# A graph layer in one kernel: node rows loaded a second time with features on partitions, their scale from a norm on TensorE, keys of block 0 and stores of counts placed earlier

## The chip, the core and the metric

One core of one Trainium2 chip. The metric is the device time of the kernel in microseconds (us), median of three runs.

## The reference, cut to what matters

6250 nodes with 128 features each, 200000 edges sorted by destination, float32. Two message layers with a residual and a normalisation each:

```python
edge_index = jnp.stack([src, dst])
h = x @ W + b_W;  xi, xj = jnp.split(h, 2, axis=-1)
xji = (xj[senders] + edge_features @ W_e + b_We) / (in_degree[receivers][..., None] + 1e-06)
x = _layernorm(x + xi + segment_sum(xji, receivers))          # layer 0
out = segment_sum(h1[src] * norm[:, None], dst) + b           # layer 1, h1 = x @ W1, self loops added
x = _layernorm(x + leaky_relu(batch_norm(out)))
```

## The kernel before

Nodes are cut into 25 blocks of 256 (`NB`), a block into 16 slots of 16 destination nodes (`SL`; the last block has 7). The gather of neighbours is a matrix product. For each slot VectorE writes one-hot tiles from the edge keys (`one_hots`, lines 616 and 619, one call for two slots, in a ring of six slots), TensorE multiplies them into counts of edges by source and destination (`count`, line 858), and ScalarE copies the counts from PSUM to SBUF (`pair_out`, line 1065, two PSUM buffers). One block later TensorE multiplies x by the counts of the whole block (`product`, line 876); one more block later come the messages, the normalisation and the second layer's first part. Edge features are summed by `edges` (line 895). Behind the 25 blocks a second sweep reads the stored counts back (`gather_z`).

x is used as two float16 halves (`xsplit`, made by `split_high` on ScalarE, line 1130, and `split_low` on VectorE, line 681). Their scale is a power of two that is read off the largest magnitude of x: `largest` (line 646, three pieces of x), `scales`, `spread_scales`. Ahead of that, x times its own weights, the own part, is made in 13 groups of up to four 128x128 tiles: `turn_x` transposes a group on TensorE (line 972), ScalarE copies it out (line 1137), `own_product` multiplies (line 981, one PSUM buffer), ScalarE copies the result into `zown` (line 1142). Groups 0 to 3 come before block 0, the others one a slot in block 0.

Work is ordered by hand. The loop `for b in range(NB + 2)` over blocks, with `for s in range(SL)` over slots inside, is written once for each engine, and each engine runs its own instructions strictly in that order, with semaphores between them. SyncE (SP) issues nearly all transfers in one queue: for a block the destination rows of block b+4 (`load_rows`), eight start values read into registers, eight small loads of edge destinations, a store of the degrees' inverse, the store of the counts of block b-1 (`keep_counts`, line 349), then the edge features in two groups (`load_edges`, line 342). Group 1 of block 0 goes into the memory where x lies, so it waits until x is split. Counts have two buffers: slot 0 of block b waits until the counts of block b-2 are stored (`counts_kept`, line 1061).

The start of a block among the sorted edges is found from destination rows: `float_rows` on ScalarE, `find_below` and `pick_rows` on VectorE, `find_rows` on TensorE, `count_row` and `start_of` on VectorE. GpSimd then gathers the block's keys (`windows`), VectorE decodes them (`make_keys`), TensorE turns them (`turn_keys`, line 921), ScalarE copies them (`tables`, line 1089).

## Time and profile before

| | |
|---|---|
| median of 3 runs | 938.35 us (937.87 to 938.45) |
| profiled execution | 936.68 us, of which the span is 934.6 us |
| TensorE busy | 883.9 us, 95% |
| VectorE busy | 676.6 us, 72% |
| ScalarE busy | 450.3 us, 48% |

The 2.1 us between the time and the span lie around the first and last recorded instruction. Shares of the whole span hide stages: the first two blocks take until about 82 us, the 25 blocks until about 715 us, and VectorE has nearly all its work in them.

### The profile page before, as it was taken

How to read it: one execution, taken by the hardware profiler on the slowest of the kernel's cores; microseconds unless marked ns; L12 is line 12 of the kernel's file. 1: busy time of each engine (PE TensorE's matmuls, PEld its weight loads, DVE VectorE, ACT ScalarE, POOL GpSimd, SP SyncE). 2: the span in 40 equal slices, each digit the busy share in tenths (PEclk: the TensorE clock that was granted, in tenths of full speed). 3: DMA queues.
4: the chain of work that ended last, by engine and by line, in shares of the span. 5: the costliest groups of instructions: out<-in, count | busy, mean ns of one | idle time of the engine just before them, and what ended most of it. 6: DMA issues, size and time to landing. Idle time of an engine off the chain costs nothing.

```text
span 934.6 us, 30500 instructions
## 1 busy us (share of the span) xinstructions
PE 883.9 (95%) x12210; PEld 791.2 (85%) x12210; DVE 676.6 (72%) x1249; ACT 450.3 (48%) x983; POOL 349.4 (37%) x401
## 2 busy tenths in 40 slices
PE   4867999999999999999999999999999999999995
PEld 4756888888988898989899999999988888888874
DVE  6999899999999998899888899888842111112255
ACT  3764666656666665556565556565542000000026
POOL 2236444455554444455334455434332011112200
PEclk8988999999999999999999999999999999999998
DMA  6428999998879788777878758678667897779654
GB/s 180 110 83 296 361 345 320 317 342 290 313 247 319 284 311 283 229 229 241 253 264 277 223 185 301 214 274 282 209 216 299 343 358 279 272 260 326 249 155 136
DMA packets 96762, 244.77 MB, mean 262 GB/s; under 512 B 39560, under 2 KB 64838, under 8 KB 90726
## 3 DMA queue, kind: packets, MB, share of 16 engines
q1 hardware_dynamic: 95014, 239.46, 73.7%
q0 software_dynamic: 1600, 3.28, 1.4%
q8 instruction: 100, 1.64, 0.8%
q14 instruction: 48, 0.39, 0.2%
HBM read 183.85 MB, written 58.85 MB: 260 GB/s over the span
## 4 chain that ended last, share of the span: by engine, by line
PE 85%; DVE 5%; issue 3%; ACT 3%; DMA 1%; SPq 1%; ACTq 0%; DVEq 0%
PE x_ps L876 26%; PE pair_ps L951 19%; PE pair_ps L858 13%; PE e_ps L895 10%; PE x_ps L884 9%; PE j_ps L933 2%; PE j_ps L981 2%; DVE lo_oh L616 1%; DVE key_oh L619 1%; PE pair_ps L960 1%; PE j_ps L934 1%; ACT counts L1065 1%; PE u_vps L1409 1%; DMA counts_kept<-counts 1%; DMA streams<-in_x 1%
## 5 line engine op out<-in xcount | busy, mean ns | idle before, releaser
L1065 ACT CAST counts<-pair_ps 128x784 bf16<-128x784 f32 x391 | 315.3, 817 | 251.5 <-PE pair_ps L858 244.1
L876 PE MATMUL x_ps<-counts,xsplit 128*128 128x256 bf16 (+1 forms) x2450 | 307.5, 271 | 0.0
L616 DVE TENSOR_TENSOR lo_oh<-counter,lo_t 128x2048 bf16<-128x2048 bf16 x196 | 252.3, 1287 | 53.9 <-PE pair_ps L858 52.5
L876 PEld LDWEIGHTS x_ps<-counts,xsplit 128*128 128x128 f16 x2450 | 222.1, 98 | 29.3 <-issue 7.1
L858 PE MATMUL pair_ps<-key_oh,lo_oh 128*128 128x100 bf16 x3128 | 207.8, 209 | 22.5 <-ACT counts L1065 15.4
L858 PEld LDWEIGHTS pair_ps<-key_oh,lo_oh 128*128 128x128 bf16 x3128 | 182.8, 98 | 36.9 <-issue 15.0
L619 DVE TENSOR_TENSOR key_oh<-counter,key_t 128x1600 bf16<-128x1600 bf16 x196 | 196.4, 1002 | 0.0
L895 PE MATMUL e_ps<-streams 128*32 128x128 f32 x3528 | 106.9, 274 | 0.1
L884 PE MATMUL x_ps<-counts,zown 128*128 128x256 bf16 (+1 forms) x840 | 105.9, 269 | 0.1
L951 PE MATMUL pair_ps<-streams,zown 128*128 128x256 bf16 x878 | 99.0, 273 | 0.0
L895 PEld LDWEIGHTS e_ps<-streams 128*32 128x32 f32 x3528 | 93.3, 110 | 4.8 <-issue 1.0
L476 POOL TENSOR_SCALAR quot<-deg 128x2 f32<-128x2 f32 x25 | 5.7, 226 | 243.2 <-DVE junk L595 231.5
L951 PEld LDWEIGHTS pair_ps<-streams,zown 128*128 128x128 f16 x878 | 85.8, 98 | 11.4 <-issue 0.2
L884 PEld LDWEIGHTS x_ps<-counts,zown 128*128 128x128 f16 x840 | 76.1, 97 | 10.3 <-issue 2.9
L492 POOL TENSOR_SCALAR bias<-linear,share 128x128 f32<-128x128 f32 x50 | 76.0, 1532 | 14.7 <-DVE vo L705 13.7
L951 PE MATMUL pair_ps<-counts,zown 128*128 128x256 bf16 (+1 forms) x732 | 79.9, 268 | 0.0
L951 PEld LDWEIGHTS pair_ps<-counts,zown 128*128 128x128 f16 x732 | 69.3, 98 | 9.2
L1313 ACT ACTIVATE u_co<-u_co 128x1 f32<-128x1 f32 x1 | 0.2, 203 | 156.0 <-DVEq L1351 156.0
L825 DVE TENSOR_TENSOR s_mem<-pair_ps,key_oh 128x256 f32<-128x256 f32 (+1 forms) x23 | 9.6, 418 | 83.8 <-PE pair_ps L951 81.3
L639 DVE TENSOR_TENSOR streams<-iota,ekeys 128x1152 f32<-128x1152 f32 x49 | 67.5, 1377 | 2.7 <-PE e_ps L895 0.3
L833 DVE TENSOR_TENSOR xsplit<-pair_ps,key_oh 128x256 f32<-128x256 f32 (+1 forms) x25 | 10.5, 419 | 58.7 <-PE pair_ps L960 57.0
L507 POOL TENSOR_TENSOR streams<-streams,key_oh 128x512 bf16<-128x512 bf16 x13 | 15.0, 1151 | 84.9 <-DMA streams<-counts_kept 84.9
(181 smaller groups left out, 890.6 us busy)
## 6 DMA issues: line engine op xcount, KB each, us to landing
streams<-in_edge_attr SPq DMA_DIRECT2D x196, 576.0 KB, 9.1
counts_kept<-counts SPq DMA_DIRECT2D x10, 1600.0 KB, 9.1
streams<-counts_kept SPq DMA_DIRECT2D x6, 1600.0 KB, 6.5
counts<-counts_kept SPq DMA_DIRECT2D x4, 1600.0 KB, 7.1
counts_kept<-counts SPq DMA_DIRECT2D x2, 3136.0 KB, 12.7
streams<-counts_kept SPq DMA_DIRECT2D x2, 3136.0 KB, 14.8
edst<-in_dst SPq DMA_DIRECT2D x196, 4.5 KB
streams<-in_x SPq DMA_DIRECT2D x3, 1024.0 KB, 5.7
```

Source lines behind the costliest of these rows:

```text
L492: last = g.tensor_scalar(bias[:, t, :], bje, share[:, 2 * b + t:2 * b + t + 1], None, ALU.mult)
L616: dv.tensor_tensor(lo_oh[:, ring, :, :, :].rearrange("p r w k t -> p (r w) k t"), counter[:, :, :].unsqueeze(1).to_broadcast([P, g, P, 2]) ...
L619: dv.tensor_tensor(key_oh[:, ring, :, :, :].rearrange("p r w k t -> p (r w) k t"), counter[:, 0:KW, :].unsqueeze(1).to_broadcast([P, g, KW ...
L639: dv.tensor_tensor(e_oh[g][:, :, :], iota[:, 0:EC].unsqueeze(1).to_broadcast([P, EG * EJ, EC]), ekeys[:, k].unsqueeze(2).to_broadcast([P, ...
L858: last = nc.tensor.matmul(pair_ps[at % 2][:, half_of, col:col + KW], lo_oh[:, at % RING, w // 2, :, w % 2], key_oh[:, at % RING, w // 2, : ...
L876: last = nc.tensor.matmul(x_ps[:, 0, 0:n], xsplit[:, q // 2, q % 2, :], by_hi[:, q // 2, :], start=(q == 0), stop=(q == 2 * HS - 1))
L884: last = nc.tensor.matmul(x_ps[:, 1, 0:n], zsplit[:, z // 2, z % 2, :], by_hi[:, z // 2, :], start=(z == 0), stop=(z == early(k) - 1))
L895: last = nc.tensor.matmul(e_ps[EC * c:EC * (c + 1), g, :], e_oh[g][:, c * EJ + j, :], ebuf[g][:, c, j, :], start=(j == 0), stop=(j == EJ - 1))
L933: nc.tensor.matmul(out, sx[:, t:m:2], wj, start=True, stop=False)
L951: last = nc.tensor.matmul(z_ps[i % 2][:, 0:n], zsplit[:, q // 2, q % 2, :], by_hi[:, q // 2, :], start=(q == early(b)), stop=(q == 2 * HS ...
L981: last = nc.tensor.matmul(j_ps[:, k, :], xT[m % 2][:, k, :], wi, start=True, stop=True)
L1065: a.copy(out.rearrange("p h (g n) -> p h g n", g=2), pair_ps[at % 2][:, :, 0:4 * KW].rearrange("p g (n h) -> p h g n", h=HI)[:, 0:HS]).the ...
```

## The change

The host lays x out twice, without arithmetic: `x_rows` as before, nodes on partitions, and `x_columns`, features on partitions, both contiguous for each partition. `x_columns` is loaded into `zown`. `own_product` takes its tiles from there, with two PSUM buffers, and its result is copied over them; `turn_x` and `x_turned` are gone, and two groups instead of four come before block 0. The scale comes from the sum of squares of x instead of its largest magnitude: `sum_squares` multiplies the upper 16 bits of each tile by themselves on TensorE (49 products into one PSUM tile), `add_squares` takes the diagonal, one product with ones adds it up and spreads it. `largest` and `spread_scales` are gone; a check over rows (`row_largest`) moves to blocks 16, 18 and 20. The rows of blocks 2 and 3 are searched before the own weights are made ready, and `turn_keys(0)` no longer has four groups of x ahead of it. `keep_counts(b - 1)` is SP's first instruction of a block instead of standing behind the loads of starts and destinations. `count_row` and `start_of` stand two slots later.

```diff
-LARGEST_AT = (None, 2, 4)
-TOP_AT, SCALES_AT, SPREAD_AT = 5, 8, 12
-HIGH_AT, LOW_AT = (11, 13, 15), (16, 18, 20)
+NORM_AT, TOTAL_AT, SCALES_AT = 9, 9, 12
+HIGH_AT, LOW_AT = (11, 13, 15), (16, 18, 21)
+ROWS_CHECKED_AT = (16, 18, 20)
 OWN = [(h, min(4, HS - h)) for h in range(0, HS, 4)]
-OWN_FIRST = 4
+SQUARED_FIRST, OWN_FIRST = 4, 2
+SQUARED_IN = {2: (4, 5, 6, 7), 6: (8, 9, 10, 11, 12)}
...
+X_TOP = 15
+ROW_LEAST = 1.0
...
+def load_pieces(sp, out, table, loaded, pieces):
     for k in pieces:
...
+        at = piece_tiles(k)
+        sp.dma_start(out[:, at.start * F:at.stop * F], table[:, at.start * F:at.stop * F]).then_inc(loaded[k], 16)
...
-        few_ps = keys_ps[:, 2:4, :]
...
-        turn_ps = [x_ps[:, :, :].rearrange("p a (b n) -> p (a b) n", n=P), e_ps]
+        own_ps = [j_ps, e_ps]
+        squares_ps, norm_ps = x_ps[:, 0, 0:P], x_ps[:, 1, 0:1]
+        upper_halves = zown[:, :].bitcast(BF16).rearrange("p (h n q) -> p h n q", n=P, q=2)[:, :, :, 1]
...
-            sp.dma_start(wi, W0[:, 0:F]).then_inc(S["wi_in"], 16)
-            load_inputs(sp, {"x": xf}, x, S, range(1))
+            load_pieces(sp, columns, x_columns, S["columns_in"], range(1))
             for b in range(2, ROW_RING):
                 load_rows(sp, b)
+            sp.dma_start(wi, W0[:, 0:F]).then_inc(S["wi_in"], 16)
             load_weights(sp, {"wj": wj, "we": we, "bi": bi, "bj": bje, "be": be_t[:, :]}, W0, b0, We, be, S)
             sp.wait_ge(win_in[0], 32)
-            load_inputs(sp, {"x": xf}, x, S, range(1, len(X_PIECES)))
+            load_pieces(sp, columns, x_columns, S["columns_in"], range(1, len(X_PIECES)))
+            load_pieces(sp, xf, x_rows, S["x_in"], range(len(X_PIECES)))
...
-                    sp.wait_ge(S["x_turned"], len(OWN))
...
+                if 1 <= b <= NB - 2:
+                    keep_counts(b - 1)
                 if b + ROW_RING < LATE:
                     load_rows(sp, b + ROW_RING)
                 if b + ROW_RING == LATE:
...
                     starts = start_values(b)
                     load_destinations(b, starts)
                     keep_inverse(b)
-                if 1 <= b <= NB - 2:
-                    keep_counts(b - 1)
...
-            def largest(k):
+            def add_squares():
+                dve.wait_ge(S["squares_summed"], 1)
+                step(dv.tensor_tensor(x1_mem[:, 0, :], squares_ps, ident[:, :], ALU.mult))
+                dv.tensor_reduce(out=norm[:, :], in_=x1_mem[:, 0, :], axis=AX.X, op=ALU.add).then_inc(S["norm_ready"], 1)
+            def scales():
+                dve.wait_ge(S["norm_out"], 1)
+                step(dv.tensor_copy(top[:, :], norm_ps))
+                dv.tensor_scalar(sound[:, 0:1], top[:, :], SQUARE_LEAST, None, ALU.is_ge)
+                dv.tensor_scalar(sound[:, 1:2], top[:, :], SQUARE_MOST, None, ALU.is_le)
+                step(dv.tensor_scalar(half_exp[:, :], top[:, :].bitcast(I32), 24, P - 1,
+                                      ALU.logical_shift_right, ALU.bitwise_and))
+                scale_i = xscale[:, :].bitcast(I32)
+                dv.tensor_scalar(scale_i[:, 0:1], half_exp[:, :], -float(ONE_EXP), float((190 + X_TOP) * ONE_EXP),
+                                 ALU.mult, ALU.add)
+                dv.tensor_scalar(scale_i[:, 1:2], half_exp[:, :], float(ONE_EXP), float((64 - X_TOP) * ONE_EXP),
+                                 ALU.mult, ALU.add).then_inc(S["scale_ready"], 1)
+                dve.wait_ge(S["scale_ready"], 1)
+            def row_largest(k):
                 at = piece_tiles(k)
...
+                step(dv.tensor_reduce(out=rowmax[:, at], in_=xsplit[:, at, 0, :], axis=AX.X,
+                                      op=ALU.max, apply_absolute_value=True))
             def check_rows():
...
+                step(dv.tensor_scalar(rowok[:, :], rowmax[:, :], ROW_LEAST, None, ALU.is_ge))
                 dv.tensor_reduce(out=total[:, 2:3], in_=rowok[:, :], axis=AX.X, op=ALU.add)
...
+                step(dv.tensor_tensor(total[:, 3:4], sound[:, 0:1], sound[:, 1:2], ALU.mult))
...
+            for b in range(2, 4):
+                find_below(b)
+                pick_rows(b)
             ready_own_weights()
             dv.memset(total[:, :], 0.0)
             step(dv.tensor_copy(ebase[:, :], ebase_i[:, :]))
-            largest(0)
             make_keys(0)
-            for b in range(2, 4):
-                find_below(b)
-                pick_rows(b)
...
                     if b == 0:
-                        if s in LARGEST_AT:
-                            largest(LARGEST_AT.index(s))
+                        if s == NORM_AT:
+                            add_squares()
                         if s == SCALES_AT:
                             scales()
-                        if s == SPREAD_AT:
-                            spread_scales()
                         if s == 3:
                             invert_degrees(0)
+                    if s == 7 and b in ROWS_CHECKED_AT:
+                        row_largest(ROWS_CHECKED_AT.index(b))
                     if SL * b + s in LOW_AT:
                         split_low(LOW_AT.index(SL * b + s))
...
-                    if s == 9 and 1 <= b < NB - 3:
+                    if s == 11 and 1 <= b < NB - 3:
                         count_row(b + 3)
-                    if s == 10 and 1 <= b < NB - 3:
+                    if s == 12 and 1 <= b < NB - 3:
                         start_of(b + 3)
...
+                if b == 0:
+                    pe.wait_ge(S["own_added"], len(OWN))
...
-            def turn_x(m):
+            def columns_here(m):
                 h, n = OWN[m]
...
-                for k in range(n):
-                    last = nc.tensor.transpose(turn_ps[m % 2][:, k, :], xrows[:, h + k, :], ident[:, :])
-                last.then_inc(S["x_turned"], 1)
+                first, last = ([end <= 2 * z for _, z in X_PIECES].index(True) for end in (h + 1, h + n))
+                for k in range(first, last + 1):
+                    pe.wait_ge(S["columns_in"][k], 16)
+            def sum_squares(m):
+                columns_here(m)
+                h, n = OWN[m]
+                for k in range(h, h + n):
+                    last = nc.tensor.matmul(squares_ps, upper_halves[:, k, :], upper_halves[:, k, :], start=(k == 0), stop=(k == HS - 1))
+                last.then_inc(S["columns_squared"], 1)
+                if m == len(OWN) - 1:
+                    pe.wait_ge(S["columns_squared"], len(OWN))
+                    pe.sem_inc(S["squares_summed"], 1)
             def own_product(m):
                 h, n = OWN[m]
+                columns_here(m)
                 pe.wait_ge(S["weights_ready"], 1)
-                pe.wait_ge(S["xT_out"], m + 1)
-                reach(pe, S["own_added"], m)
+                reach(pe, S["own_added"], m - 1)
                 for k in range(n):
-                    last = nc.tensor.matmul(j_ps[:, k, :], xT[m % 2][:, k, :], wi,
-                                            start=True, stop=True)
+                    last = nc.tensor.matmul(own_ps[m % 2][:, k, :], own[:, h + k, :], wi, start=True, stop=True)
                 last.then_inc(S["own_done"], 1)
-            for b in range(2):
+            for b in range(ROW_RING):
                 find_rows(b)
-            for m in range(OWN_FIRST):
-                turn_x(m)
-                if m >= 1:
-                    own_product(m - 1)
+            for m in range(SQUARED_FIRST):
+                sum_squares(m)
+                if m < OWN_FIRST:
+                    own_product(m)
             turn_keys(0)
-            for b in range(2, 4):
-                find_rows(b)
-            own_product(OWN_FIRST - 1)
             pe.wait_ge(S["starts_known"], 2)
             for b in range(NB + 2):
                 u = b - 2
...
                     if b < NB and s < slots(b):
                         count(b, s)
                     if b == 0:
-                        if s == TOP_AT:
...
-                        if s == SCALES_AT + 1:
...
-                        if OWN_FIRST <= OWN_FIRST + s - 1 < len(OWN):
-                            own_product(OWN_FIRST + s - 1)
+                        for m in SQUARED_IN.get(s, ()):
+                            sum_squares(m)
+                        if s == TOTAL_AT:
+                            pe.wait_ge(S["norm_ready"], 1)
+                            nc.tensor.matmul(norm_ps, ones[:, :], norm[:, :], start=True, stop=True).then_inc(S["norm_out"], 1)
                         if OWN_FIRST + s < len(OWN):
-                            turn_x(OWN_FIRST + s)
+                            own_product(OWN_FIRST + s)
                     if s == 1 and 0 <= u < NB:
                         messages(u)
                     if s == 3 and 1 <= b < NB - 3:
                         find_rows(b + 3)
-                    if b == 1 and s == 3:
-                        pe.wait_ge(S["scale_ready"], 1)
...
+                act.wait_ge(S["x_in"][k], 16)
                 a.activation(xsplit[:, at, 0, :], xrows[:, at, :], ACT.Copy,
                              scale=xscale[:, 0:1]).then_inc(S["x_high"], 1)
...
             def own_out(m):
                 h, n = OWN[m]
                 act.wait_ge(S["own_done"], m + 1)
-                a.copy(own[:, h:h + n, :], j_ps[:, 0:n, :]).then_inc(S["own_added"], 1)
+                reach(act, S["columns_squared"], m + 1)
+                a.copy(own[:, h:h + n, :], own_ps[m % 2][:, 0:n, :]).then_inc(S["own_added"], 1)
...
-            for m in range(OWN_FIRST):
-                x_turned(m)
-                if m >= 1:
-                    own_out(m - 1)
             for b in range(2, 4):
                 float_rows(b)
+            for m in range(OWN_FIRST):
+                own_out(m)
...
-            own_out(OWN_FIRST - 1)
             root_degrees(0)
             for b in range(NB + 2):
                 u = b - 2
...
                             early_sums(u)
                     if b < NB and s < slots(b):
                         pair_out(b, s)
-                    if b == 0 and OWN_FIRST <= OWN_FIRST + s - 1 < len(OWN):
-                        own_out(OWN_FIRST + s - 1)
                     if b == 0 and OWN_FIRST + s < len(OWN):
-                        x_turned(OWN_FIRST + s)
+                        own_out(OWN_FIRST + s)
...
+def x_layouts(np, x):
+    tiles = np.zeros((HS, P, F), x.dtype)
+    whole = (NB - 1) * BN
+    tiles[0:HS - 1] = x[0:whole].reshape(NB - 1, P, 2, F).transpose(0, 2, 1, 3).reshape(HS - 1, P, F)
+    for half in range(2):
+        tiles[HS - 1, 64 * half:64 * half + LAST_P] = x[whole:].reshape(LAST_P, 2, F)[:, half]
+    return [np.ascontiguousarray(tiles.transpose(order)).reshape(P, HS * F) for order in ((1, 0, 2), (2, 0, 1))]
```

TensorE, from its first instruction to the first count of block 0 (line 858 before, 838 after). Before:

```order
L911 MATMUL pair_ps<-rows,pick 128x129 x2
L972 MATMUL x_ps<-ident,streams 128x128 x4
L972 MATMUL e_ps<-ident,streams 128x128 x4
L981 MATMUL j_ps<-linear,x_mem 128x128 x4
L972 MATMUL x_ps<-ident,streams 128x128 x4
L981 MATMUL j_ps<-linear,s_mem 128x128 x4
L972 MATMUL e_ps<-ident,streams 128x128 x4
L981 MATMUL j_ps<-linear,x_mem 128x128 x4
L921 MATMUL keys_ps<-ident,key 128x128
```

After (`sum_squares` is line 955, `own_product` 967, `turn_keys` 903):

```order
L893 MATMUL pair_ps<-rows,pick 128x129 x4
L955 MATMUL x_ps<-zown 128x128 x4
L967 MATMUL j_ps<-linear,zown 128x128 x4
L955 MATMUL x_ps<-zown 128x128 x4
L967 MATMUL e_ps<-linear,zown 128x128 x4
L955 MATMUL x_ps<-zown 128x128 x8
L903 MATMUL keys_ps<-ident,key 128x128
```

The keys of block 0 had three groups of own products and four groups of transposes ahead of them; now they have two groups of own products and 16 square products.

SP, in block 1, from the last edge load of block 0 on. Eight start values and eight destination loads are cut to one row each. Before:

```order
L342 DMA streams<-in_edge_attr 128x1152
L301 DMA rows_i<-in_dst 128x129
L327 TENSOR_LOAD estart_i
...
L333 DMA edst<-in_dst 128x9
L370 DMA dinv_rows<-dinv 128x2
L349 DMA counts_kept<-counts 128x12544
```

After, the store is line 338:

```order
L331 DMA streams<-in_edge_attr 128x1152
L338 DMA counts_kept<-counts 128x12544
L290 DMA rows_i<-in_dst 128x129
L317 TENSOR_LOAD estart_i
...
L323 DMA edst<-in_dst 128x9
L359 DMA dinv_rows<-dinv 128x2
```

It stands ahead of the row load, the start values and the eight destination loads, which it followed.

## Rows read from the trace of the kernel before

**Rows 1.** Busy time, share of the span and instructions of TensorE, VectorE and ScalarE

```profile
PE 883.9 (95%) x12210; PEld 791.2 (85%) x12210; DVE 676.6 (72%) x1249; ACT 450.3 (48%) x983; POOL 349.4 (37%) x401
```

**Rows 2.** Windows: busy us of PE, PEld, DVE, ACT, POOL; PEclk, DMA share, GB/s

```profile
20.00:30.00 10.00, 7.75 (x68) 6.97 (x67) 10.00 (x21) 6.39 (x11) 2.06 (x3) 0.73 0.08 7
...
100.00:200.00 100.00, 97.19 (x1588) 87.30 (x1587) 96.97 (x176) 67.30 (x142) 47.91 (x55) 1.00 0.94 331
...
400.00:600.00 200.00, 199.73 (x3067) 181.70 (x3066) 175.34 (x314) 119.36 (x243) 91.82 (x102) 1.00 0.75 248
```

**Rows 3.** Timeline, start and length in us, up to the first one-hot of block 0

```profile
6.34 0.28 DVE L688 TENSOR_TENSOR linear<-linear,ident 128x128 f32<-128x128 f32 x1
...
7.16 0.29 DVE L691 TENSOR_SCALAR linear<-linear,lmean 128x128 f32<-128x128 f32 x1
...
9.93 2.01 PE L981 MATMUL j_ps<-linear,x_mem 128*128 128x128 f32 x8
...
11.14 0.23 DVE L582 TENSOR_SCALAR bit_i<-gsrc 128x128 int32<-128x128 int32 x1 [0.75 <-DMA gsrc<-in_src,start_i]
...
12.70 0.29 DVE L602 TENSOR_TENSOR lo<-lo_i,upper 128x128 bf16<-128x128 int32 x1
...
16.25 0.30 ACT L1151 ACTIVATE heads<-rows_i,shift 128x2 f32<-128x2 int32 x1
...
17.22 0.25 ACT L1089 CAST key_t<-keys_ps 128x128 bf16<-128x128 f32 x1
...
17.98 0.35 DVE L562 SCALAR_TENSOR_TENSOR pick<-even,heads,below 128x128 bf16<-128x128 f32 x1
...
19.54 1.22 DVE L616 TENSOR_TENSOR lo_oh<-counter,lo_t 128x2048 bf16<-128x2048 bf16 x1
```

**Rows 4.** DMA issues at 2.1 and 3.7 us: KB each, us from issue to landing

```profile
streams<-in_x SPq DMA_DIRECT2D x1, 1024.0 KB, 5.9
...
linear<-in_L_gnn_W SPq DMA_DIRECT2D x1, 64.0 KB, 4.6
```

**Rows 5.** Timeline of block 0, one slot and the first split of x

```profile
21.80 0.82 PE L858 MATMUL pair_ps<-key_oh,lo_oh 128*128 128x100 bf16 x8 [1.37 <-DVE key_oh L619]
...
29.48 1.13 PE L981 MATMUL j_ps<-linear,x_mem 128*128 128x128 f32 x8 [0.41 <-ACT x_mem L1137]
...
30.99 0.53 PE L858 MATMUL pair_ps<-key_oh,lo_oh 128*128 128x100 bf16 x8
...
31.82 1.13 PE L981 MATMUL j_ps<-linear,s_mem 128*128 128x128 f32 x8 [0.30 <-issue]
...
46.45 2.01 ACT L1130 ACTIVATE xsplit<-streams,xscale 128x2048 f16<-128x2048 f32 x1
```

**Rows 6.** Instructions of line 646: duration in ns, least, median, most

```profile
L646 DVE TENSOR_REDUCE rowmax<-streams x3: 2277/2286/2411, 8.1 to 29.7; 128x16 f32<-128x2048 f32 x2, 128x17 f32<-128x2176 f32 x1
```

**Rows 7.** Timeline around the store of block 0's counts

```profile
63.72 1.91 SPq L342 DMA_DIRECT2D streams<-in_edge_attr  x4
...
75.47 0.43 SPq L349 DMA_DIRECT2D counts_kept<-counts  x1
...
87.80 1.53 ACT L1065 CAST counts<-pair_ps 128x784 bf16<-128x784 f32 x2 [5.61 <-issue]
```

**Rows 8.** DMA issue at 75.5 us: KB, us to landing

```profile
counts_kept<-counts SPq DMA_DIRECT2D x1, 3136.0 KB, 12.3
```

**Rows 9.** Two windows of block 2; sum of seven from 80 to 114 us

```profile
85.00:90.00 5.00, 1.25 (x11) 1.10 (x12) 5.00 (x5) 1.91 (x3) 4.56 (x4) 0.69 0.98 403
...
105.00:110.00 5.00, 5.00 (x97) 4.54 (x87) 2.93 (x5) 2.54 (x7) 0.00 (x0) 1.00 0.94 397
...
sum 34.00, PE 28.29 PEld 24.89 DVE 29.57 ACT 19.22 POOL 14.11; mean PE 4.04 PEld 3.56 DVE 4.22 ACT 2.75 POOL 2.02
```

**Rows 10.** Timeline of ScalarE: end of block 2, slot 10 of block 3

```profile
112.12 0.49 ACT L1073 ACTIVATE sx<-x_ps,xscale 128x256 f32<-128x256 f32 x1
...
127.82 0.30 ACT L1151 ACTIVATE heads<-rows_i,shift 128x2 f32<-128x2 int32 x1
```

**Rows 11.** DMA issues of the whole span: count, KB each, median us to landing

```profile
rows_i<-in_dst SPq DMA_DIRECT2D x23, 64.5 KB, 7.4
```

95 lines of the change are left out of this document (18 added, 77 removed).

## The prediction

> **What bounds the kernel now.** I read the shares first, then windows by stage, then the waits and the timeline of the stages that differ. The page gives TensorE 95% of the span and VectorE 72% [rows 1], which hides that the early blocks have another limit. By windows, VectorE is busy 10.00 of 10 us in block 0 and 96.97 of 100 in blocks 3 to 6, where TensorE is near its limit too (97.19); from 400 us on TensorE has 199.73 of 200 and VectorE 175.34 [rows 2]. So work taken off VectorE, or an earlier start of its chain, counts up to about 200 us; behind that only what arrives as a shift of TensorE's whole stream counts, and nothing later gives it back, because TensorE has no waits there to absorb one.
>
> Three places come before that stream.
>
> First, the start. The gathered keys are there at 11.14 us and decoded at 12.99 (12.70 and 0.29), but TensorE turns them only later and ScalarE copies them at 17.22, and the first one-hot is built at 19.54 [rows 3]. What lies between are the own groups in front of them on TensorE and ScalarE and the row search of blocks 2 and 3.
>
> Second, block 0. One slot there takes 2.34 us (from the own product at 29.48 to the next at 31.82), a loop of TensorE (transposes, own product 1.13, counts 0.53) and ScalarE (two copies and the counts) with one buffer for the product [rows 5]. From 19.54 to the first split of x at 46.45 are 26.9 us [rows 3, 5].
>
> Third, block 2. ScalarE stands still for 5.61 us until 87.80 us. The trace names no engine. Slot 0 of block 2 needs the counts of block 0 stored, and that store is issued at 75.47 and lands 12.3 us later, at 87.8 [rows 7, 8]: that is the wait. The store was possible long before, but SP waited until 63.72 for the memory of x and then issued rows, starts and destinations first [rows 7].
>
> **The change, part by part.**
>
> *Start (term A).* The gathers are issued as before, so keys are decoded at about 13.0. The first piece of columns is issued where the weights were, half a microsecond earlier than x's at 2.1, and x's took 5.9 [rows 4], so it lands at 7.0 to 7.6. The loads behind it land right with it: the weights issued at 3.7 landed 4.6 later, 0.3 behind x [rows 4]. So rows 2 and 3 and the own weights come at about 7.6. The search of those two blocks took 2.1 us (16.25 to 18.33) and the weights 1.1 (6.34 to 7.45) [rows 3], so they are done at 9.7 and 10.8, both ahead of the keys. TensorE then has 16 squares and two own groups ahead of the keys. An own group takes 2.01 at the start and 1.13 later [rows 3, 5]. For a square I find no row; the nearest is a count, eight products in 0.82 slow or 0.53 fast, 0.07 to 0.10 each [rows 5], 1.1 to 1.6 for 16. From 10.8: 2.0 + 1.1 to 2.0 + about 1.3 + 0.4 for the keys' turn is 15.6 to 16.5; 0.5 for ScalarE's two copies of 0.25 gives the first one-hot at 16.1 to 17.0. I take 16.9, for gaps between them: 2.6 us earlier than 19.54. Bounds: 1.0 (both groups slow, squares double) to 4.5 (keys straight after decoding).
>
> *Block 0 (term B).* Removed: nine slots' worth of transposes and their copies; VectorE's second and third `largest` at 2.29 and 2.41 [rows 6] and the wait for the scales to come back. (The first `largest` lay in a wait for keys and was worth nothing.) Added: 33 squares at 0.07, 2.3 us, one tiny product, five small VectorE instructions. Without the removed copy between transpose and product, TensorE's slot is product and counts: 1.13 + 0.4 to 0.53, say 1.55, and ScalarE's two copies take less. Slots 0 to 10 with 11 groups, the last of one tile: 2 slow slots of 2.7 and 2.0, eight of 1.55, one of 0.8, 2.3 of squares, 0.4 of keys and norm, together 20.6. Ahead of it 2.2 for the first pair of one-hots, behind it 2.2 of ScalarE until the first split: 25.0 instead of 26.9, so 1.9 earlier. VectorE will now wait about 4 us for the squares of slot 6, but its pair for slot 12 still comes in time; the norm is known some 2 us before ScalarE wants it. Bounds: 0.5 (slots at 1.7) to 4.5 (a slot at 1.4, near TensorE's busy share of it, and squares hidden). ScalarE's splits (2.01 each) [rows 5] and VectorE's stay the pace of slots 11 to 18, and VectorE's stream of block 1 stays: the shift is carried.
>
> *Store of the counts (term C).* SP issues it right behind the edges of block 0, at 65.7 (63.72 and 1.91) instead of 75.5 in the old clock [rows 7], so it lands at 78.0, before slot 0 of block 2 needs it at 82.2 (87.80 less the 5.61 waited). ScalarE's 5.61 us go. But VectorE goes on during that stall, and its stream is next in line at block 3. From 80 to 114 us it is busy 29.57 of 34.00, idle 4.4, of which 2.1 in one window [rows 9]; it cannot come forward by more. I take 3.7, since some short waits will stay; bounds 2.0 and 4.4.
>
> *Hidden.* `row_largest`: three reductions as long as the old, 2.3 us each [rows 6], in blocks 16 to 20, where VectorE has 12% left and runs several slots ahead [rows 2]; without that cover up to 7 us. The second copy of x is 3.1 MB more to load in the first 27 us; x_rows is not read before about 42. The check at the end has TensorE's sweep over it. The store's wait for the last slot now holds back rows, destinations and edges of a block by 1 to 2 us; edges issued then are used a block later.
>
> Sum: 2.6 + 1.9 + 3.7 = 8.2 us. The profiled execution took 936.68, which gives 928.5; that execution was 1.7 below the median of the runs, and from the median it is 938.35 - 8.2 = **930.1 us**.
>
> **A rule that speaks against it.** The row load of block b+4 now stands directly behind a 3136 KB store. In the rows, row loads land in 7.4 [rows 11], the store in 12.3 [rows 8], and ScalarE wants the rows 15.7 after the block's start (112.12 to 127.82) [rows 10]. Taken as behind the whole store they come after some 13 us, 2 to 3 before they are wanted, so I price this at nothing. The Trainium skill, "DMA: Bandwidth & Descriptors", section "Queues, rings and completion order", says that on each DMA engine the transfers of one issuing engine are taken in ring order, so the rows would indeed wait for the store's data. By that rule the term stays zero as long as the store lands in under 15; no row here shows a row load in that place.
>
> **Rivals.**
> - *Only the stall goes.* The own weights come late (their load moved behind four others), the two own groups hold TensorE up ahead of the keys, and VectorE's wait for the squares delays block 0's pairs. Against it: the loads land together by [rows 4]. A + B fall to 0.5: 938.35 - 4.2 = 934.2.
> - *The stall moves to VectorE.* In the window of the stall VectorE is busy 5.00 of 5 [rows 9]. If its idle time in [rows 9] is only made of waits that recur, C is 1 or less: 938.35 - 4.5 - 1 = 932.9.
> - *More.* Block 0 at its lower bound for slots and a start near 16: A + B = 7.5, with C 11.2: 927.2.
> - *Slower.* The rows' landing behind the store. If stores take 12.3 alone but 19 when edges of both groups share the queue, the rows come 3.3 us after ScalarE wants them; two slots of buffer (2.5 us) leave 0.8 a block on TensorE's path, over 17 blocks 13.6, less 8.2: 943.8. It decides from a landing of about 18.7 on, where 0.5 a block eats the 8.2. For it: DMA share 0.94 to 0.98 in these windows [rows 2, 9]. Against: 2.5 to 3 us to spare in every block.
> - *No change*, within 0.2%, 1.9 us, which is what a measurement of this kernel tells from nothing: the first two rivals together.
>
> **How the numbers follow.** Forecast 0.55 (928 to 932.5), only the stall 0.15, stall moved 0.11, more 0.08, no change 0.04, slower 0.07. From 926.5 to 935 holds the forecast, most of the two smaller gains and most of "more", some 0.83. Faster by over 0.2% are the first four: 0.89.
>
> **What would show it.** First one-hot at 16 to 17.5; first split of x at about 42; no wait of ScalarE for the store in block 2, and block 2's `sx` copy at about 77; messages of block 3 some 8 us earlier than before, and the same shift at 400 and 700 us. Wrong it would be by ScalarE waiting for `rows_i`, TensorE for own weights ahead of the keys, or VectorE's idle time in block 2 unchanged.

## The result: slower by 1.0%, and where the profile after shows the loss

The changed kernel takes 946.76 us in the median of 4 runs (945.80 to 949.57) where the kernel before takes 938.11 (937.54 to 938.45). The ratio is 1.0096, with a 95% interval of 1.0073 to 1.0120: slower by some 9 us, where 8.2 less were forecast. The profiled execution took 946.37 us, its span is 944.6.

The shares, in the page's first row, hide it as they did before:

```profile
PE 882.1 (93%) x12209; PEld 789.4 (84%) x12209; DVE 675.7 (72%) x1245; ACT 444.1 (47%) x970; POOL 388.1 (41%) x400
```

TensorE's busy time is 1.8 us less than in [rows 1], yet the span is 10.0 us longer, so the difference is idle time. The windows (columns as in [rows 2]) say in which part:

```profile
20.00:30.00 10.00, 9.89 (x127) 9.59 (x125) 7.81 (x19) 8.04 (x14) 4.91 (x5) 0.95 0.85 237
60.00:80.00 20.00, 9.64 (x160) 8.44 (x161) 12.90 (x17) 5.38 (x10) 10.27 (x8) 0.89 0.95 283
80.00:114.00 34.00, 28.28 (x412) 24.52 (x410) 25.82 (x47) 17.05 (x36) 12.74 (x14) 0.91 0.83 289
100.00:200.00 100.00, 89.47 (x1416) 79.64 (x1413) 88.52 (x165) 61.05 (x125) 49.94 (x51) 0.98 0.93 302
400.00:600.00 200.00, 199.36 (x3063) 181.38 (x3062) 179.24 (x314) 119.39 (x244) 102.89 (x98) 1.00 0.79 249
```

Two of the same windows in the kernel before:

```profile
60.00:80.00 20.00, 17.27 (x310) 15.25 (x311) 19.90 (x25) 9.73 (x16) 14.48 (x11) 1.00 0.59 170
80.00:114.00 34.00, 28.29 (x421) 24.89 (x420) 29.57 (x61) 19.22 (x39) 14.11 (x17) 0.90 1.01 374
```

Block 0 is better (9.89 of 10 us on TensorE against 7.75, and a granted clock of 0.95 against 0.73), the late blocks are as before. TensorE is busy only 9.64 us of the 20 from 60 to 80 (17.27 before) and 89.47 of the 100 from 100 to 200 (97.19 in [rows 2]); from 80 to 114, where the kernel before has its stall of 5.61 us, it is busy no longer than there.

**The gains are there, and larger than forecast.** Timeline of the start and of the first split of x:

```profile
12.84 1.80 PE L967 MATMUL e_ps<-linear,zown 128*128 128x128 f32 x8
...
14.93 0.22 PE L903 MATMUL keys_ps<-ident,key 128*128 128x128 f16 x1
...
15.71 1.22 DVE L604 TENSOR_TENSOR lo_oh<-counter,lo_t 128x2048 bf16<-128x2048 bf16 x1 [1.91 <-ACT lo_t L1065]
...
38.16 2.01 ACT L1106 ACTIVATE xsplit<-streams,xscale 128x2048 f16<-128x2048 f32 x1
```

The first one-hot comes 3.8 us earlier than in [rows 3] and the first split 8.3 earlier than in [rows 5].

**Block 1 loses them.** SyncE's DMA issues, then ScalarE and TensorE:

```profile
55.41 2.07 SPq L331 DMA_DIRECT2D streams<-in_edge_attr  x4
57.52 0.43 SPq L338 DMA_DIRECT2D counts_kept<-counts  x1
58.00 0.46 SPq L290 DMA_DIRECT2D rows_i<-in_dst  x1
...
77.04 0.30 ACT L1122 ACTIVATE heads<-rows_i,shift 128x2 f32<-128x2 int32 x1 [11.95 <-DMA rows_i<-in_dst]
...
78.47 0.83 PE L838 MATMUL pair_ps<-key_oh,lo_oh 128*128 128x100 bf16 x8 [7.61 <-ACT counts L1040]
```

The row load of block 5 is issued at 58.00 behind the store and lands 19 us later. ScalarE, whose instructions run in order, stands 11.95 us in front of it, the copies of the counts stand behind it, and TensorE waits 7.61 for them. In the kernel before the same load was issued at 65.69 and used at 73.34, here in the timeline of ScalarE:

```profile
73.34 0.30 ACT L1151 ACTIVATE heads<-rows_i,shift 128x2 f32<-128x2 int32 x1
```

Block 1 had 7.65 us for it, not the 15.7 of block 3 [rows 10].

**Block 2 gives nothing back.** The wait of 5.61 us for the count buffer [rows 7] is gone, but TensorE stops in the middle of an edge group, between instructions that have no semaphore wait between them:

```profile
101.19 1.50 PE L877 MATMUL e_ps<-streams 128*32 128x128 f32 x45
...
106.45 1.92 PE L877 MATMUL e_ps<-streams 128*32 128x128 f32 x27 [3.75 <-issue]
```

From the view of waits of the whole span (us in total, times, longest):

```profile
PEld pair_ps L838 <- issue: 26.6, 21, 7.9
...
ACT heads L1122 <- DMA rows_i<-in_dst: 18.6, 6, 12.0
...
PEld e_ps L877 <- issue: 9.7, 8, 4.0
```

Of the 18.6 us of ScalarE, 4.0 in two waits lie in the start, before 8 us. Before, ScalarE's waits for `rows_i` were 0.4 in all, TensorE's loads of counts waited for "issue" 15.0, those of edges 1.0.

The copies of `sx`, one for each block, show it as a running sum. Start of a copy, in us against the kernel before (single profiled executions; kernels are explained below):

| copy of `sx` | 1st | 2nd | 6th | 12th | 25th |
|---|---|---|---|---|---|
| before, us | 81.69 | 112.12 | 212.63 | 370.69 | 713.91 |
| changed | +2.73 | +2.84 | +5.95 | +8.46 | +8.58 |
| r3, before with early store | +12.47 | +5.43 | +12.22 | +16.38 | +17.53 |
| r1, store back | -10.63 | -11.84 | -9.96 | -8.86 | -9.13 |
| r2, rows first | -8.37 | -7.95 | -2.22 | +0.44 | +1.73 |
| r4, early in block 1 only | -8.14 | -7.97 | -8.16 | -5.62 | -5.89 |
| r10, r2 with keys ahead | -11.30 | -13.56 | -8.87 | -4.87 | -4.28 |
| r6, r4 with keys ahead | -10.37 | -14.57 | -13.25 | -10.56 | -10.72 |
| r9, r1 with keys ahead | -11.77 | -12.77 | -13.51 | -12.91 | -13.18 |

Block 1 turns -8.3 into +2.7, which is 11.0 us; the blocks up to the 12th copy lose 5.7 more. The rest of the 10.0 is behind the last copy: 222.1 us against 220.7.

### The profile page after: what moved, and what is told of

It is laid out like the page before. It is cut to its first block, busy times and chain, and to the rows that moved or that the text cites. A ratio compares the mean times of both kernels' runs of the same rounds, so it can differ in the third digit from the quotient of the medians.

```text
span 944.6 us, 30473 instructions
## 1 busy us (share of the span) xinstructions
PE 882.1 (93%) x12209; PEld 789.4 (84%) x12209; DVE 675.7 (72%) x1245; ACT 444.1 (47%) x970; POOL 388.1 (41%) x400
## 3 DMA queue, kind: packets, MB, share of 16 engines
q8 instruction: 100, 1.64, 0.7%
## 4 chain that ended last, share of the span: by engine, by line
PE 86%; DMA 3%; issue 3%; DVE 3%; ACT 3%; SPq 0%; ACTq 0%; DVEq 0%
PE x_ps L856 27%; PE pair_ps L933 17%; PE pair_ps L838 14%; PE e_ps L877 11%; PE x_ps L864 9%; DMA rows_i<-in_dst 2%; PE j_ps L915 2%; ACT counts L1040 1%; PE j_ps L916 1%; DMA key_oh<-sums_z 1%; PE pair_ps L942 1%; PE u_vps L1375 1%; PE j_ps L967 1%; PE e_ps L967 1%; ACT u_xo L1294 1%
## 5 line engine op out<-in xcount | busy, mean ns | idle before, releaser
L604 DVE TENSOR_TENSOR lo_oh<-counter,lo_t 128x2048 bf16<-128x2048 bf16 x196 | 247.7, 1264 | 61.9 <-PE pair_ps L838 59.6
L838 PE MATMUL pair_ps<-key_oh,lo_oh 128*128 128x100 bf16 x3128 | 208.0, 209 | 28.9 <-ACT counts L1040 18.6
L607 DVE TENSOR_TENSOR key_oh<-counter,key_t 128x1600 bf16<-128x1600 bf16 x196 | 199.3, 1017 | 0.0
L877 PE MATMUL e_ps<-streams 128*32 128x128 f32 x3528 | 109.9, 275 | 8.5 <-issue 7.2
L482 POOL TENSOR_TENSOR bias<-bias,linear 128x256 f32<-128x256 f32 x25 | 51.5, 2059 | 2.1
```

Of the source, the lines that this page charges most:

```text
L482: g.tensor_tensor(bias[:, :, :], bias[:, :, :], bi.unsqueeze(1).to_broadcast([P, 2, F]), ALU.add).then_inc(S["bias_ready"], 1)
L604: dv.tensor_tensor(lo_oh[:, ring, :, :, :].rearrange("p r w k t -> p (r w) k t"), counter[:, :, :].unsqueeze(1).to_broadcast([P, g, P, 2]) ...
L607: dv.tensor_tensor(key_oh[:, ring, :, :, :].rearrange("p r w k t -> p (r w) k t"), counter[:, 0:KW, :].unsqueeze(1).to_broadcast([P, g, KW ...
L838: last = nc.tensor.matmul(pair_ps[at % 2][:, half_of, col:col + KW], lo_oh[:, at % RING, w // 2, :, w % 2], key_oh[:, at % RING, w // 2, : ...
L877: last = nc.tensor.matmul(e_ps[EC * c:EC * (c + 1), g, :], e_oh[g][:, c * EJ + j, :], ebuf[g][:, c, j, :], start=(j == 0), stop=(j == EJ - 1))
```

## The experiments

My theory had two parts: the row load is late because it stands behind the store in SyncE's queue (theory 1), and the early store delays other things in every block (theory 2). The rivals were the new start, the longer wait of SyncE, and DMA engines that are full whatever the order. Ratios are to the kernel before, run on the same chip, with 95% intervals; 0.1% is 0.94 us. Not all kernels ran on the same chip, so they are compared with each other by these ratios. Of each edit only the lines that matter are shown, and the comments in them are mine.

### r1: the store back at its old place

```
+                if 1 <= b <= NB - 2:          # last of SyncE's steps, as before
+                    keep_counts(b - 1)
```

> The changed kernel with one part undone: the counts store of block b-1 is issued again where it was before the change, last of SyncE's steps in a block, behind the row load, the starts, the destination loads and the inverse store. Theory 1 (the row load of block 5 sits behind the store in SyncE's queue, lands 19 us after its issue and stalls ScalarE by 12 in block 1): that stall goes, the copy of sx at the end of block 1 comes some 8 us before that of the kernel before (81.69), near 73.5, and the wait of block 2 for the count buffer (5.6 us) is back. Time near 938.1 - 8.3 = 929.8, range 928.5 to 932. Theory 2 (something else of the start, the new order of block 0's work or the heavier GpSimd, takes the time in block 1): the stall stays, 943 to 947. Theory 3 (the moved store costs little by itself, its backlog in the queues is what delays later blocks): as theory 1, and the differences of block starts also stay at -8 from block 2 on.

931.37 us, ratio 0.9946 (0.9927 to 0.9966), runs from 929.2 to 934.3. The stall of block 1 is gone and that of block 2 is back (ScalarE 5.1 us). So the rest of the change is a gain of some 5 us, and the moved store alone turned it into a loss.

### r2: the row load first, the store second

```
                 if b + ROW_RING < LATE:
                     load_rows(sp, b + ROW_RING)
+                if 1 <= b <= NB - 2:
+                    keep_counts(b - 1)
```

> The changed kernel with two of SyncE's steps exchanged: in every block the row load is issued first, then the counts store, then starts, destinations and the inverse store. Theory 1 (the place behind the store is the whole loss): the row load lands some 7 us after its issue as before, ScalarE's wait of 12 goes, and so do the smaller ones of blocks 3 to 5; both the 5.6 of block 2 and the 8.3 of the start are kept, time 924 to 928. Theory 2 (the early store's transfer fills the DMA queues, and instruction fetches, edge loads and destination loads behind it come late): the wait of block 1 goes, but TensorE's pauses without a wait (named issue) of blocks 2 to 9 stay, and the time is 5 or more above that, 930 to 935, with the copies of sx drifting later from block to block against the kernel before.

936.10, ratio 0.9976 (0.9956 to 0.9995). ScalarE's waits for `rows_i` fall from 18.6 to 4.4 us, of which 3.7 lie in the start and 0.64 in block 1, and 11 us are back. But this is not better than r1: 1 us above theory 2's 930 to 935, far from theory 1's 924 to 928. In the table the lead of 8 us is kept until the 2nd copy and used up by the 12th.

### r3: only the store moved, all else as before

> The kernel before with only one of the change's parts: the counts store of block b-1 is issued first of SyncE's steps in block b. Theory 1: block 1 stalls as in the changed kernel where the row load comes late. SyncE's steps of block 1 are held up by x in both kernels, so the row load is issued near 65.7 and lands 12 to 19 us later, 78 to 85, against a want at 73.3: a loss of 5 to 11, of which block 2 gives back up to 5.6. With the drift of later blocks (5 us between blocks 2 and 9 of the changed kernel) the time is 940 to 948. If the drift belongs to the start's new order and not to the store: 938 to 943. If the early store is harmless by itself: 932 to 936.

953.47, ratio 1.0178 (1.0156 to 1.0201): worse than I gave any theory room for. The row load, issued at 67.60, comes 11.69 us too late for ScalarE. The store costs 17 us here and 14 between r1 and the changed kernel, so the loss hangs on the store and not on the new start.

### r4: rows first, and the early store in block 1 alone

```
+                if b == 1:                    # behind load_rows
+                    keep_counts(b - 1)
...
+                if 2 <= b <= NB - 2:          # at the old place
+                    keep_counts(b - 1)
```

> As the kernel with rows first, but the early store is made in block 1 alone; from block 2 on the store stands last again, as in the kernel before. Theory 1: nothing but block 1's order matters, so the time is that of the kernel with rows first, within 1 us (924 to 928). Theory 2 (the early store of every block costs later blocks something): this kernel is 3 to 8 us faster than the one with rows first, 924 to 928 against 930 to 935. If the wait for the count buffer returns in block 3 (its store, of block 1, is late again), some 2 to 5 us are lost there: 928 to 932.

929.75, ratio 0.9916 (0.9896 to 0.9936), 0.6% below r2 with intervals apart. Theory 2 holds, though the gain is 5.6 us and the time not as low as 924 to 928 (in block 3 of this execution there is no wait for the count buffer, so the third case of the expectation is not the reason): the early store of blocks 2 and on only costs.

### r5: SyncE's wait early, the transfer late

```
+                if 1 <= b <= NB - 2:
+                    sp.wait_ge(S["pair_out"], first_slot(b - 1) + slots(b - 1))
                 if b + ROW_RING < LATE:
```

> The kernel with the store back at its old place, plus one thing of the moved store without its transfer: at the start of each block SyncE waits, ahead of the row load, until ScalarE has stored the last counts of block b-1. Theory 2a (what the early store costs is its transfer of up to 3.1 MB, behind which row loads, gathers and TensorE's instructions come late): no change against the kernel with the store back, 928 to 933. Theory 2b (it is SyncE being held by the wait, so that row loads, starts and destination loads are issued late): a part of the 10 to 15 us between that kernel and the changed one comes back, 936 to 944, with row loads issued late and landing some 7 us after their issue.

933.84, ratio 0.9955 (0.9939 to 0.9970) beside r1's 0.9946: no difference that can be told. It is the transfer that costs, not SyncE's wait, which I had named among the hidden costs at 1 to 2 us a block.

### r7: store first, row loads in ScalarE's own queue

```
+                    if s == 0 and b >= 1 and b + ROW_RING < LATE:
+                        load_rows(act, b + ROW_RING)
```

> The changed kernel, store first as in it, but the row loads of blocks 5 and later are issued by ScalarE at the start of each block, in its own queue, not by SyncE behind the store. If the row load was late because it stands behind the store in SyncE's queue (ring order): it lands within some 8 us of its issue, ScalarE's wait of 12 in block 1 is gone, and the time is that of the kernel with rows first, 934 to 938. If it was late because the transfers share the same 16 engines whatever queue they come from: it still lands 12 us or more after its issue, ScalarE waits several us in block 1, and the time is 940 to 947.

938.40, ratio 1.0008 (0.9986 to 1.0030), 0.3% above r2 with intervals that overlap, and 0.9% below the changed kernel. It doesn't tell the two apart, though: ScalarE reaches slot 0 of block 1 early and issues the load at 43.46, 15 us ahead of the store at 58.25. So this is rows first by another way, and r13 had to follow.

### r13 and r14: one row load just behind the store in time, in another queue

```
+                if b != 1 and b + ROW_RING < LATE:   # SyncE, ahead of load_rows
...
+                    if b == 1 and s == 7:            # ScalarE
+                        load_rows(act, b + ROW_RING)
```

> The changed kernel, with one row load changed: that of block 5 is issued in block 1 by ScalarE at slot 7, near 59 us, so some 1 us behind the store of 3136 KB in time, but in another queue than SyncE's. All other row loads stay behind the store in SyncE's queue. If the load was late because of the order within SyncE's queue: it lands 7 to 9 us after its issue, near 67, and ScalarE waits 1 to 3 us at slot 10 where it waited 12; the time is 935 to 941. If it was late because all 16 engines were busy with what was issued before it, in whatever queue: it lands near 76, ScalarE waits 9 or more, and the time is 943 to 948.

> Control for the kernel before it: the same row load by ScalarE at slot 7 of block 1, with all stores at their old place, so that no store is in transfer there. The load should land within 8 us by either theory, with 1 to 2 us of wait or none at slot 10; if it waits as long as in the other kernel, it is the edge loads and not the store that the load stands behind. Time 929 to 936.

The rows that decide, r13's (store, load, use) and then r14's, which has no store in transfer there:

```profile
58.46 0.43 SPq L338 DMA_DIRECT2D counts_kept<-counts  x1
...
59.06 0.38 ACTq L290 DMA_DIRECT2D rows_i<-in_dst  x1
...
71.36 0.30 ACT L1122 ACTIVATE heads<-rows_i,shift 128x2 f32<-128x2 int32 x1 [5.28 <-DMA rows_i<-in_dst]
...
101.29 0.30 ACT L1122 ACTIVATE heads<-rows_i,shift 128x2 f32<-128x2 int32 x1 [7.49 <-DMA rows_i<-in_dst]
```

```profile
57.66 0.38 ACTq L290 DMA_DIRECT2D rows_i<-in_dst  x1
...
64.85 0.30 ACT L1122 ACTIVATE heads<-rows_i,shift 128x2 f32<-128x2 int32 x1 [0.18 <-issue]
```

The same load takes 19.0 us behind the store in one queue, 12.3 beside it in another (59.06 to 71.36), and at most 7.2 without it. In these three executions the order within the queue costs about 7 us and the busy engines 5; my expectation had it as one or the other. In r14 the edge loads are in transfer as well, so they alone don't hold the load up in block 1. In block 2 it is otherwise: in r1, with no store early, the row load issued at 74.62 takes 15.1 us, and in r4 one issued at 76.89 takes 14.1. There it is wanted only 17 to 19 us after its issue.

The time surprised more: 946.01 for r13, ratio 1.0088 (1.0062 to 1.0113), no better than the changed kernel, though its first copy of `sx` is 7.6 us earlier. The row above names the next place. In block 2 the row load, still behind the store in SyncE's queue, is issued at 79.15 and used at 101.29, and ScalarE waits 7.49 there. In the changed kernel ScalarE comes to this place at 100.88 (issue at 84.66) and does not wait; r13 comes to it at 93.80. So the stall of block 1 had given the load of block 2 its slack. By the 12th copy r13 is 6.4 behind the kernel before. So "11 us in block 1" is where the changed kernel pays, not what one repair there would give back. r14 took 932.23, ratio 0.9923 (0.9894 to 0.9952), like r1.

### r8: the store in two halves, one early, one late

```
+                mid = (at + n) // 2 // 256 * 256
+                c = slice(at, mid) if part == 0 else slice(mid, n)
```

> The kernel with rows first, but the store of a block's counts in two halves of about 1.6 MB (contiguous in each partition): one at the early place, one at the old place, behind the destination loads and the inverse store. If the loss against the store at its old place grows with what is in transfer early in the block: TensorE's pauses without a wait are between those of rows first (8.4 us over 6 pauses in blocks 1 to 12) and store back (3.2), and the time is between theirs, 930 to 935. If it is any early store that does it: 935 to 938. If two smaller transfers let others through, as well as half the wait for the count buffer in block 2 goes: 926 to 930.

935.89, ratio 0.9975 (0.9957 to 0.9994), the same as r2. As far as intervals of 0.2% to either side can tell, half the bytes early cost as much as all of them; TensorE's pauses over 0.5 us are 4.8 us in 3 of them, against 8.4 in r2, so they alone don't account for the time.

### r6: block 0's keys turned ahead of the second own product (on r4)

```
             for m in range(SQUARED_FIRST):
                 sum_squares(m)
                 if m < OWN_FIRST:
                     own_product(m)
+                if m == 0:
+                    turn_keys(0)
```

and on ScalarE `tables(0)` between the first and the second `own_out`.

> The kernel with the store early in block 1 only, and in TensorE's and ScalarE's start the turn of block 0's keys and their copies put ahead of the second own product and squares 1 to 3. In the changed kernel the keys are decoded at 12.5 and turned at 14.93, behind own products of 2.05 and 1.80, and the first one-hot starts at 15.71. The turn can start near 12.9, so the first one-hot near 13.8, 1.9 us sooner, if VectorE's other start work (ready by 13.8) does not hold it: 927.5 to 928.5 against 929.75. If ScalarE's copies or the one-hots are what block 0 waits for anyway, or the own products only come back as a wait a few slots later: same as that kernel, 929 to 930.5.

924.39, ratio 0.9858 (0.9842 to 0.9875): the best here, and 5.4 us below r4, not 1.9. The first one-hot starts where it was expected:

```profile
12.76 0.27 PE L905 MATMUL keys_ps<-ident,key 128*128 128x128 f16 x1
...
13.87 1.21 DVE L606 TENSOR_TENSOR lo_oh<-counter,lo_t 128x2048 bf16<-128x2048 bf16 x1
```

A part of the rest is the clock. TensorE no longer stands still for 2.78 us ahead of the first counts. The windows from 15 to 20 us (length, PE busy and count, granted clock, DMA share, GB/s), first of the changed kernel, then of r6 (there with all engines: PE, PEld, DVE, ACT, POOL):

```profile
15.00:20.00 5.00, 2.22 (x18) 0.77 1.01 424
```

```profile
15.00:20.00 5.00, 5.00 (x61) 4.77 (x61) 5.00 (x18) 3.57 (x7) 0.05 (x1) 1.00 1.02 426
```

The first split of x comes at 35.12 here and at 38.01 in r4: 2.9 us, 1 more than the keys alone give. A second part comes in block 2. There r4 has a granted clock of 0.75 from 80 to 85 us and 0.56 from 85 to 90, behind a wait of 1.92 for one-hots and a pause of 0.72, and its 72 products of edges take 4.07 us; r6 has 1.00 in both windows and 2.17 us for the same products. By the second copy of `sx` it leads r4 by 6.6 us. Each is a single execution, and why the clock held in r6 is not shown.

Nine of the kernels (the changed one, r1, r2, r4, r5, r7, r8, r13, r14) share the start with the pause of 2.78 us. In the profiles of eight of them the granted clock was 0.66 to 0.93 from 20 to 25 us; in r1's it was 1.00, with the first split of x 1.9 to 3.3 us earlier than in the others. So the same start can go either way. That this is what spreads the runs of r1, r2, r5, r7 and r8 (5 to 10 us from the least to the most) is not shown: r11, which has no such pause, spreads by 7.5 us in five runs.

### r9, r10, r11: the three orders again, on the start of r6

> The kernel with block 0's keys ahead (924.4), but with every counts store at its old place, last of SyncE's steps, in block 1 too. If the early store in block 1 saves what it was made for (the wait of block 2 for the count buffer, 5.1 us in the kernel with the store back): 927 to 930. If the transfer cannot land sooner in block 1 whatever its place, since edge loads and the store need the DMA engines for some 14 us there (it landed at 76.45 when issued at 57.8, and at 76.67 when issued at 66): 923.5 to 926.

r9, all stores at the old place: 928.09, ratio 0.9905 (0.9890 to 0.9920). By the ratios of r9 and r6 the early store in block 1 is worth 4.4 us, the first of my two cases. r12 below, which has r6's order of stores and ran on r9's chip, makes it 3.2. ScalarE's wait for the count buffer, in the view of waits from 60 to 90 us, r9 and then r6:

```profile
ACT counts L1041 <- issue: 5.4, 1, 5.4
```

```profile
ACT counts L1043 <- issue: 1.6, 1, 1.6
```

r9's profiled execution, 924.86, was the fastest of its four, r6's, 926.92, the slowest; one profile against another would have given the opposite answer. In the table r6 leads r9 by 1.8 us at the second copy of `sx` and by nothing from the 6th on, so the traces show the shorter wait, but not that it lasts to the end: that rests on the medians of four runs each.

> The kernel with keys ahead, row load first and the store second in every block, not in block 1 alone. If the early store costs later blocks through what its transfer delays (6.4 us between the medians of rows first and of the store early in block 1 alone, both with a start that varies by several us): 929 to 933 here too, with more pauses of TensorE without a wait in blocks 3 to 12. If that difference came of the varying start: 924 to 926.

r10, the early store in every block: 930.89, ratio 0.9920 (0.9905 to 0.9935), 5.8 us above r6 by the ratios and 4.6 above r12. One of its five executions took 1806.61 us and is not in the ratio; the median of the other four is 930.48. The program has a general form for other inputs behind the fast one; whether that execution ran it, and why it took so long, is open.

The pauses now have a cause. In 12 of the 14 kernels with the new start TensorE stops for over 0.5 us at the same instruction, behind the same six products, a few us ahead of the 6th copy of `sx`, and how long it stops is what differs (r5 has 0.27 us there, the changed kernel no stop to be seen). Timeline, r9 and then r10:

```profile
193.00 0.82 PE L856 MATMUL x_ps<-counts,xsplit 128*128 128x256 bf16 x6
194.66 0.38 PE L856 MATMUL x_ps<-counts,xsplit 128*128 128x256 bf16 x2 [0.84 <-issue]
```

```profile
192.36 0.82 PE L856 MATMUL x_ps<-counts,xsplit 128*128 128x256 bf16 x6
197.67 0.38 PE L856 MATMUL x_ps<-counts,xsplit 128*128 128x256 bf16 x2 [4.49 <-issue]
```

The view of DMA traffic, cut to quarters of a microsecond (queue, packets, MB, share of 16 engines), has one packet of the instruction queue, 0.02 MB, ahead of each such restart. In r9 from 192.25 and in r10 from 195.25:

```profile
q8 instruction: 1, 0.02, 25.2%
```

```profile
q8 instruction: 1, 0.02, 23.8%
```

In r9 TensorE goes on 2.4 us after 192.25, in r10 2.4 after 195.25, in the changed kernel 2.4 after one at 104.00 (the pause that ends at 106.45), and in the kernel before 2.4 after one at 205.00, with a pause of 1.24 at another instruction. It holds for all of them: the 16 profiles together have 69 pauses of TensorE over 0.5 us that the trace puts down to no releaser, behind 12 us, and before every one of them such a packet starts, in 64 of them 2.2 to 2.65 us before TensorE goes on, in the other five 2.85 to 4.2 us before. With 100 packets in some 930 us that is no coincidence. In r10 the packet comes 3.6 us later relative to TensorE's own work than in r9 (from 192.36 and 193.00), where the store is in transfer early, and the pause is 3.65 us longer.

The Trainium skill, "Runtime: NRT & Kernel Launch", section "Instruction fetch mechanics", says that a sequencer refills its instruction memory in blocks of 16 KiB through a DMA queue of its own, mostly hidden. The size agrees: the page of each profile has 100 packets and 1.64 MB in this queue. Most are hidden here too, since only 1 to 8 pauses over 0.5 us stand against the 100 packets of a run, but those that are not cost up to 4.49 us.

The pauses up to 400 us add up as theory 2 has it: 0.8 to 4.3 us in the eight kernels where no store or only that of block 1 is early, 4.8 to 11.6 in the eight where it is early in every block. Between r2 (8.4) and r4 (3.3) they differ by 5.2 of the 5.6 us, between r10 (8.3) and r6 (2.7) by 5.6 of the 5.8. r8, with 4.8 us of pauses and r2's time, does not fit.

> The changed kernel (946.8: the store first and the row load behind it in every block) with only block 0's keys put ahead of the second own product. Theory 1: the 12 us wait of ScalarE for the row load of block 5 stays in block 1, and may grow by what the start is sooner, so 940 to 946; against the kernel with rows first and keys ahead it is 10 or more slower.

r11, store first as changed: 947.13, 1 us above the expected range, ratio 1.0086 (1.0055 to 1.0117). Against r10 the place of one 64.5 KB row load in each block is worth 1.7%, 15.6 us; ScalarE waits 17.9 us for `rows_i` in 7 places against 4.5 in 3 (3.5 and 3.6 of it in the start). The gain of 5 us that the keys bring elsewhere is wholly swallowed.

### r12: the starts of later blocks again at slots 9 and 10

> The kernel with keys ahead and the early store in block 1 alone, with one small part of the change undone: VectorE's count of the row and start of block b+3 at slots 9 and 10 again, in place of 11 and 12. Nothing waits for these starts within a block, so no change: 923.5 to 925.5. If they hold VectorE where TensorE waits for its one-hots (PE waits for key_oh 2 us in block 2): 1 to 2 us either way.

925.84, ratio 0.9871 (0.9854 to 0.9888) beside r6's 0.9858: no change to be told.

## Why the prediction was wrong, point by point

By ratios, the changed kernel divides into: start and block 0 -0.54% (r1), the early store in block 1 with rows first -0.30% (r4 less r1, intervals that overlap; -0.47% between r9 and r6), the early store in all later blocks +0.60% (r2 less r4), the row load behind the store +1.20% (changed less r2). Together +0.96%, some 9 us. They are differences from one kernel to the next, so the sum must come out; what they tell is the size of each, with an interval of some 0.2% to either side.

- **The step that failed** is the price of nothing for the row load, "ScalarE wants the rows 15.7 after the block's start (112.12 to 127.82) [rows 10]". That was read in block 3. In block 1 SyncE is held by x until 63.72 [rows 7], so the load had 7.65 us, and landed 7.5 after its issue: there was no slack at all. With the store in front it took 19. The rival *Slower* named this mechanism and put its deciding point at a landing of 18.7, but priced it on 17 blocks at 0.8 each, held that there were 2.5 to 3 us to spare in every block, and gave it 0.07. It came as 11.0 us in block 1; the later waits for rows are 2.7 us in three places (4.0 more lie in the start), and would be more without the first (r13). Its 943.8 is near the measured 946.76 by luck: one block paid, not 17.
- **Landing time of the store.** The row of 12.3 [rows 8] was taken as the store's own. In r4 it is issued at 57.8, right behind four edge loads of 576 KB and one row load, and lands 18.6 later. The DMA share there is 0.95 or more in every window of 2 us from 58 to 72. I had the range for that, in the same rival, and weighed it too low.
- **Not in the sum at all:** what the transfer does to traffic that isn't in SyncE's order, above all TensorE's instructions. 5.6 us between r2 and r4, 5.8 between r10 and r6. The pauses show a mechanism of the right size; that they are the whole of it is not shown (r8).
- **Term A**, 2.6, measured 3.8 in the trace: the row search and weights were done as worked out, but four of the 16 squares ran before the weights were there (from 9.47), and the gaps I allowed for weren't there (keys turned at 14.93, one-hot at 15.71 against 16.9).
- **Term B**, 1.9, measured 4.5 in the trace. The 2.2 us ahead of the slots and the 2.2 behind them came as worked out (2.3 and 2.2); slots 0 to 10, 20.6 in the sum, took 18.0. The term that was mis-sized is the slot of own product and counts: 1.32 us (31.52 to 32.84 in the changed kernel), against 1.55 for eight of them, which is 1.8 of the 2.6 us. The two slow slots took 4.1 against 4.7. The windows show the granted clock of 20 to 30 us at 0.95, from 0.73 [rows 2].
- **A and B together**, forecast 4.5, are 8.3 at the first split but 5.1 in the medians (r1). Some is lost behind the last copy of `sx`, where all kernels with the new start take 221.1 to 223.0 us and those without it 220.4 and 220.7; why is open. I put the rest down to executions that differ, which is not shown.
- **Term C**, 3.7, is right in mechanism and near in size where the row load stands ahead of the store and only block 1's store is early: 4.4 (r9 to r6), 3.2 (r9 to r12), 2.8 (r1 to r4, intervals that overlap). But the store lands 18.4 to 18.6 us after its issue (r6, r4) and not 12.3, so a wait of 1.6 to 3.7 us stays, where the sum had it gone. The limit of 4.4 by VectorE's idle time [rows 9] was not tested.
- *Only the stall goes* and *the stall moves to VectorE* did not happen as such; in r4, TensorE waits 1.92 us for VectorE's one-hots in block 2, a piece of the latter.

## What to carry to other kernels

Before a large transfer is moved ahead, list the small ones behind it and find for each the block in which it has least time between issue and use, not a typical one; the first blocks, where a queue is held by something else, are where it breaks. Move it where a wait is known, in one block, and not everywhere; and expect a stall that is repaired to show up again in the next block that lived on its slack. Put a short step that starts a long chain (here the turn of the keys) ahead of longer ones that nobody waits for yet, and when a pause of TensorE is avoided, look at the granted clock behind it: what was lost there can be more than the pause.

## What the runs showed of the hardware

- In block 1 a load of 64.5 KB took 19.0 us behind a 3136 KB store in the same queue (changed kernel), 12.3 beside it in another (r13), 7.2 or less without it (r14); in block 2 it took 15.1 with no early store at all (r1). The first agrees with the ring order that the Trainium skill gives under "DMA: Bandwidth & Descriptors", section "Queues, rings and completion order". In r4, GpSimd's gather issued at 64.48 was used at 75.68, and VectorE waited 1.37 us for it; it took 3.7 in the kernel before.
- The 3136 KB store landed 12.3 us after its issue in the kernel before (75.47) and 18.6 in r4 (57.8, right behind four edge loads).
- TensorE stops for its own instructions, 0.57 to 4.49 us at one and the same instruction in 12 kernels, longest where the store is in transfer early; it goes on 2.2 to 2.65 us after the packet starts, in 64 of 69 pauses.
- After such a pause the granted clock is low: 0.65 from 204 to 208 us in r2 (pause 2.48), 0.57 from 106 to 110 in the changed kernel (pause 3.75), 0.64 from 197 to 201 in r10 (pause 4.49). After one of 0.84 in r9 it is 1.00 from 194 to 198.
- With the same start and the same pause of 2.78 us near 15 us, the granted clock behind it was 0.66 to 0.93 in eight profiles and 1.00 in one (r1).
